# Output projection of a cross-attention layer in three fp32r passes, with reordered selections, maxima and remainders

## The reference

```python
def xattn(query, key, value, mask, ...):      # query = layernorm(x), key = value = ctx
    q = query @ Wq + bq                       # 16 heads of 16
    k = key @ Wk + bk                         # one head of keys and values for all
    v = value @ Wv + bv
    scores = einsum('bhqd,bkd->bhqk', q, k) / sqrt(16)
    scores = where(mask == 0, -1e9, scores)
    x = einsum('bhqk,bkd->bhqd', softmax(scores), v)
    return x @ Wo + bo                        # the output projection

def ffn(x, ...):                              # x = layernorm(x1)
    x_mixed = mix_kernel[0] * previous row + mix_kernel[1] * row + mix_kernel[2] * next row
    h = einsum('bsd,pdm->bspm', x_mixed, W1) + b1             # 9 paths of 64
    stacked = einsum('bspm,pmd->bspd', h, W2) + b2
    idx = argmax(tanh(x_mixed @ Wo1 + bo1) @ Wo2 + bo2)       # one path per row
    return layernorm(x + stacked[idx]) * gamma + beta

x1 = x + xattn(layernorm(x), ctx, ctx, mask)
out = x1 + ffn(layernorm(x1))
```

## Time and profile before

| | before |
|---|---|
| median of 3 runs | 339.88 us (339.84 to 340.29) |
| the profiled execution | 341.15 us, of which the span of instructions is 339.3 us |
| TensorE busy | 306.1 us, 90% of the span |
| VectorE busy | 269.8 us, 80% |
| GpSimd busy | 194.1 us, 57% |
| ScalarE busy | 178.8 us, 53% |
| mean granted TensorE clock | 0.986 |

### The profile page before, as it was taken

The page is one execution under the profiler, slowest core; times in us unless marked ns, Lnnn a source line. Parts: engine busy times, 40 slices in busy tenths (PEclk is TensorE's granted clock), DMA queues, the critical chain, the costliest instruction groups (busy, mean ns, idle before and its releaser), DMA issues. The chain is left out here.

```text
span 339.3 us, 7009 instructions
## 1 busy us (share of the span) xinstructions
PE 306.1 (90%) x2700; PEld 224.0 (66%) x2700; DVE 269.8 (80%) x620; ACT 178.8 (53%) x279; POOL 194.1 (57%) x235
## 2 busy tenths in 40 slices
PE   1688978779899999999999999999999999899991
PEld 1563355365578766795778766795779578766891
DVE  2786698898769797989789797979598868495876
ACT  1354715814861686537842777357462655356620
POOL 0264001493196289925895299827884597519554
PEclk9999699999999999999999999999999999999998
DMA  7942200002002001200120010000100010001003
GB/s 218 231 103 68 77 2 1 2 1 79 3 6 74 2 2 62 77 3 0 65 65 16 0 63 2 2 0 3 64 2 1 0 65 2 0 2 43 22 0 124
DMA packets 20586, 13.14 MB, mean 39 GB/s; under 512 B 10113, under 2 KB 20426, under 8 KB 20554
## 3 DMA queue, kind: packets, MB, share of 16 engines
q1 hardware_dynamic: 18914, 12.14, 11.9%
q10 hardware_dynamic: 1640, 0.57, 0.7%
HBM read 8.51 MB, written 4.19 MB: 37 GB/s over the span
## 5 line engine op out<-in xcount | busy, mean ns | idle before, releaser
L1507 POOL TENSOR_TENSOR rs<-ve,halfneg 128x4 f32<-128x4 f32 x22 | 25.1, 1142 | 80.7 <-DVE ve L1155 80.7
L894 ACT ACTIVATE e<-ps 128x1024 f32<-128x1024 f32 x32 | 31.1, 1023 | 17.6 <-PE ps L577 17.6
L1192 DVE TENSOR_REDUCE mx<-ps 128x16 f32<-128x1024 f32 x32 | 38.0, 1214 | 0.3 <-PE ps L545 0.3
L1595 POOL TENSOR_TENSOR hml<-hs,hmh 128x512 fp32r<-128x512 f32 x28 | 35.0, 1277 | 5.3 <-ACT hmh L956 5.3
L700 PE MATMUL ps<-w2h,hmh 128*128 128x256 f32 (+1 forms) x140 | 35.6, 289 | 0.0
L701 PE MATMUL ps<-w2l,hmh 128*128 128x256 f32 (+1 forms) x140 | 34.6, 283 | 0.0
L946 ACT ACTIVATE hs<-ps,b1s 128x512 f32<-128x512 f32 x28 | 19.3, 689 | 23.4 <-PE ps L452 23.4
L613 PE MATMUL ps<-wo,osb 128*128 128x256 f32 x128 | 31.4, 391 | 0.0
L1312 DVE TENSOR_TENSOR hs<-hs,ps 128x512 f32<-128x512 f32 x28 | 18.5, 681 | 15.7 <-PE ps L680 15.7
L919 ACT ACTIVATE xh<-x,vb,rs 128x256 f32<-128x256 f32 x24 | 12.5, 590 | 33.0 <-POOL vb L1520 33.0
L1560 POOL TENSOR_TENSOR y<-xh2f,gms 128x256 f32<-128x256 f32 x24 | 20.4, 878 | 15.9 <-DVE xh2f L1164 15.9
(11 more groups left out here) (169 smaller groups left out, 772.5 us busy)
## 6 DMA issues: line engine op xcount, KB each, us to landing
xin<-in_x SPq DMA_DIRECT2D x8, 512.0 KB, 3.8
out<-y SPq DMA_DIRECT2D x6, 512.0 KB, 2.8
min_<-in_mask_Bx1xSxS_ik SPq DMA_DIRECT2D x8, 128.0 KB, 4.0
hs<-in_L_ffn_W SPq DMA_DIRECT2D x2, 288.0 KB
hs<-in_L_ffn_W SPq DMA_DIRECT2D x1, 512.0 KB
out<-y SPq DMA_DIRECT2D x2, 256.0 KB, 2.1
out<-xin SPq DMA_DIRECT2D x2, 256.0 KB, 2.3
cst<-in_constants SPq DMA_DIRECT2D x1, 384.0 KB, 6.6
```

Source lines behind the costliest of these rows:

```text
L894: nc.scalar.activation(e[:, 2 * i:2 * i + 2, :], ps[:, bank:bank + 2, :], ACT.Exp).then_inc(s_e, 1)
L1192: v.tensor_reduce(mx[:, k, :].rearrange("p (a h) -> p a h", a=2), ps[:, bank:bank + 2, :].rearrange("p a (h s) -> p a h s", s=SK), AX.X, A ...
L1507: g.tensor_tensor(ln[7][:, :], ln[6][:, :], halfneg[:, :], ALU.pow).then_inc(s_r, 1)
L1595: g.tensor_tensor(L.lo(m, r), L.selected(m, r), L.hi(m, r).bitcast(F32), ALU.subtract).then_inc(L.s_hl, 1)
```

## The change

It does the following:
1. The projection is made in three fp32r passes. Wo is split once (`woh` on ScalarE at the end of step 1, `wol` on GpSimd). The attention output is rounded in halves on ScalarE (`attn_hi`) and its remainder made on VectorE (`attn_lo`); TensorE waits for the one ahead of the first two products of a tile and for the other ahead of the third. They lie in buffers of the tail (`lhh`, `lhl`).
2. On TensorE `rep3` stands ahead of the projection of tiles 0 and 1, and `scores_for_max` of tiles 2 and 3 inside W2, behind the hi products of tiles 0 and 2. On VectorE all selections stand ahead of the first maximum, and the last two maxima behind the x1 sums.
3. GpSimd's remainder of the mix stands behind `rstd2`.
4. In full steps q is rounded on ScalarE, not on VectorE. `keep_xh2` stands behind the roundings of the selections.
5. The variance of the usual layer norms is made by aggregation (`bn_aggr` per tile and two small operations) in place of six operations.

```diff
             def project_out(b, j, tiles):
-                pe.wait_ge(s_oT, at(b, 2 * NJ, 2 * j + tiles[0] // 2 + 1))
+                half = at(b, 2 * NJ, 2 * j + tiles[0] // 2 + 1)
+                if (b, j) == (0, 0):
+                    pe.wait_ge(s_wol, 1)
+                pe.wait_ge(s_oTh, half)
                 for k in tiles:
+                    o, ks = ps[:, k // 2, (k % 2) * D:(k % 2 + 1) * D], slice(k * P, (k + 1) * P)
                     for c in range(KD):
-                        mm = nc.tensor.matmul(ps[:, k // 2, (k % 2) * D:(k % 2 + 1) * D], osb[:, c, k * P:(k + 1) * P],
-                                              wo[:, c, :], start=(c == 0), stop=(c == KD - 1))
+                        nc.tensor.matmul(o, osh[:, c, ks], woh[:, c, :], start=(c == 0), stop=False)
+                        nc.tensor.matmul(o, osh[:, c, ks], wol[:, c, :], start=False, stop=False)
+                    pe.wait_ge(s_oTl, half)
+                    for c in range(KD):
+                        mm = nc.tensor.matmul(o, osl[:, c, ks], woh[:, c, :], start=False, stop=(c == KD - 1))
                 mm.then_inc(s_wo, 1)
...
+            def attn_hi(b, j):
+                for half in range(2):
+                    act.wait_ge(s_oT, at(b, 2 * NJ, 2 * j + half + 1))
+                    t = slice(half * CH // 2, (half + 1) * CH // 2)
+                    nc.scalar.activation(osh[:, :, t], osb[:, :, t], ACT.Copy).then_inc(s_oTh, 1)
...
                 if f:
                     hidden(*f, 2)
                     hidden(*f, 3)
+                    selected_hi(*f, 0)
+                    attn_hi(*n)
+                    for m in range(1, NM):
+                        selected_hi(*f, m)
                     keep_xh2(*f)
-                    for m in range(NM):
-                        selected_hi(*f, m)
...
-                v.tensor_tensor(su, st[:, :, 0, :], st[:, :, 1, :], ALU.add)
-                v.tensor_tensor(dm, st[:, :, 0, 1], st[:, :, 1, 1], ALU.subtract).then_inc(s_halves, 1)
...
+                for k in tiles:
+                    a = v.bn_aggr(ln[1][:, k, :], ln[0][:, k].rearrange("p a c -> p (a c)"))
...
+            def attn_lo(b, j, half):
+                dve.wait_ge(s_oTh, at(b, 2 * NJ, 2 * j + half + 1))
+                t = slice(half * CH // 2, (half + 1) * CH // 2)
+                v.tensor_tensor(osl[:, :, t], osb[:, :, t], osh[:, :, t].bitcast(F32), ALU.subtract).then_inc(s_oTl, 1)
...
-                if f and f[1] == 0:
-                    mixed_lo(f[0], 1)
-                if f and n[1] == NJ - 1:
-                    early_mixed_lo(n[0])
                 if front and front[1] == 0:
                     value_operand(front[0])
...
                 if n:
                     rstd2(*n)
+                if f and f[1] == 0:
+                    mixed_lo(f[0], 1)
+                if f and n[1] == NJ - 1:
+                    early_mixed_lo(n[0])
```

More of the change, by code:

```diff
@@ L174, in layer_program @@
         lhh, lhl = sb("lhh", [P, NM - 1, CH], F32R), sb("lhl", [P, NM - 1 - KD, CH], F32R)
+        osh, osl = lhh[:, 0:KD, :], lhh[:, KD:2 * KD, :]
+        woh, wol = [lhl[:, i, :].rearrange("p (c n) -> p c n", c=KD) for i in range(2)]
         wq32 = h4s[:, :].rearrange("p (c n) -> p c n", c=KD)
@@ L764, in step @@
                 if f:
-                    rep(*f, 3)
-                    if front:
-                        scores_for_max(*front, 2, banks)
                     rep(*f, 4)
@@ L770, in step @@
                     project_out(*n, (2, 3))
-                if f and front:
-                    scores_for_max(*front, 3, banks)
-                if f and front:
-                    w2_tiles(*f, (0, 1, 2, 3))
-                elif f:
+                if f:
                     w2_product(*f, 0, "hi")
                     w2_product(*f, 2, "hi")
+                if f and front:
+                    scores_for_max(*front, 2, banks)
+                    scores_for_max(*front, 3, banks)
+                if f:
                     w2_product(*f, 0, "lo")
@@ L781, in step @@
                     w2_product(*f, 2, "lo")
+                if f and front:
+                    w2_tiles(*f, (3,))
                 if front:
@@ L989, in step @@
                     pv_copy(*n)
+                if front and f:
+                    q_round(*front)
                 if f:
@@ L992, in step @@
                     hidden(*f, 3)
+                    selected_hi(*f, 0)
+                    attn_hi(*n)
+                    for m in range(1, NM):
+                        selected_hi(*f, m)
                     keep_xh2(*f)
-                    for m in range(NM):
-                        selected_hi(*f, m)
                 if after and not f:
                     layernorm1_apply(*after)
+                if n and not f:
+                    attn_hi(*n)
                 if late and not f:
@@ L1001, in step @@
                     copies_t1(*after, 6, False, 1)
+                    act.wait_ge(s_wo_in, 32)
+                    nc.scalar.activation(woh, wo[:, :, :], ACT.Copy).then_inc(s_woh, 1)
                 if f:
+                    act.wait_ge(s_xh2f, at(f[0], NJ, f[1] + 1))
                     layernorm2_apply(*n)
@@ L1232, in x1_stats @@
                 if half:
-                    variance(ln2, (s_ln2s, s_ln2h, s_ln2p, s_ln2v), c, 2 * c, -1.0)
+                    variance(ln2, (s_ln2s, s_ln2p, s_ln2v), c, 2 * c, -1.0)
             def mix(b, j, last, sems):
@@ L1340, in residual_stats @@
                 if half:
-                    variance(ln3, (s_ln3s, s_ln3h, s_ln3p, s_ln3v), c, 2 * c)
+                    variance(ln3, (s_ln3s, s_ln3p, s_ln3v), c, 2 * c)
             def tail_variance(i, stats, sign=1.0):
@@ L1373, in step @@
                     early_mix(n[0])
-                if front:
+                if front and not f:
                     q_round(*front)
@@ L1391, in step @@
                     select(*f, 1)
+                if n:
+                    attn_lo(*n, 0)
+                if f:
                     select(*f, 2)
+                if n:
+                    attn_lo(*n, 1)
+                if f:
+                    select(*f, 3)
+                    select(*f, 4)
                     if front:
@@ L1395, in step @@
                         take_max(*front, 1, banks)
-                    select(*f, 3)
-                    select(*f, 4)
-                    if front:
-                        take_max(*front, 2, banks)
                     if n:
@@ L1403, in step @@
                     if front:
+                        take_max(*front, 2, banks)
                         take_max(*front, 3, banks)
```

30 lines of the change are left out of this document (16 added, 14 removed).

## The result

The changed kernel takes 346.34 us (median of 4 runs, 345.44 to 348.2), the kernel before 339.86 us beside it (339.34 to 340.29). The ratio is 1.0199, with a 95% interval of 1.0169 to 1.023: slower, by about 2% (the interval has 2% in its middle). The prediction was 349.4 us, with a range of 339.5 to 354.0.

What follows compares the result with a forecast made beforehand. TensorE, 90% busy, waits on VectorE's chain to the variance, which has 0.8 us of cover. 6.0 (full steps) + 2.8 (steps 2, 3) + 0.7 (step 9) = 9.5 on 341.15 gives 350.6, less 1.27: 349.4 us, range 339.5 to 354.0.

Steps and rivals of the forecast that it cites:

- the two mechanisms: VectorE's two-input operations wait for GpSimd passes at two places per full step: attention remainders, 0.9 us; maxima split, +0.34 us.
- rival 1: VectorE's attention remainders don't wait for GpSimd, only the split of the maxima does: +4.3 us, 344.2 us; chance 0.20.
- TensorE's saving: Three-pass projection on TensorE: 0.75 us less per chunk, 6.0 us over 8 at most, swallowed by waiting for the maxima.
- s: Instant in a step when TensorE spreads the inverse denominators; the forecast counts the step's later events from it.
- x: Instant when VectorE ends the second layer norm's variance: s + 11.2 without any collision, s + 12.1 forecast.
- First collision: Full step, ahead of the variance: VectorE's two attention remainders wait for GpSimd's selection remainders, 0.9 us, bounds 0 and 2.5.
- Second collision: Full step, behind the variance: the maxima split waits for GpSimd's moved mix remainder, +0.34 us, bounds -0.7 and about +0.8.
- A full step: A step with selections and scores (steps 4 to 8): 0.9 + 0.34 = 1.2 us longer, +6.0 us for five.
- Steps 2 and 3: Steps without selections: both attention remainders precede VectorE's last two maxima, +1.4 us each, +2.8; bounds per step -0.75 and +2.2.
- Step 9: The step without scores, where every delay of the variance counts in full: +0.7 us, within -0.3 and +1.6.
- Rival 2: VectorE goes first each time and GpSimd waits: -0.9 us, 339.0 us, or 334.7 with TensorE's saving; chance 0.20.
- Rival 3: A later maxima split delays following work into the next step, some 1.2 us more in four steps: 354 us; chance 0.10.

Runs made afterwards that it cites:

- e4: The changed kernel with GpSimd's remainder of the selections made for 16 of 512 columns only, from the second chunk on: 344.11 us in one run.
- e1: The changed kernel with GpSimd's remainder of the mix back at the front of its step: 343.37 us.
- e8: The changed kernel with VectorE's two attention remainders ahead of selections 1 to 4, the mix remainder left where the change puts it: 345.37 us.
- e5: e1 with VectorE's two attention remainders ahead of selections 1 to 4 and replications 3 and 4 behind the projection's first half: 341.71 us.
- e9: e6 with the residual and its statistics one maximum earlier on VectorE, and the fourth score tile behind W2's second tile: 338.05 us.
- e6: e5 with the first batch's output projections in fp32, without attention rounding and remainders there: 339.27 us.
- e3: The changed kernel with the projection in plain fp32, without the roundings and remainders of the attention output: 342.58 us.
- e7: e3 with GpSimd's remainder of the mix at the front of its step: 339.08 us.
- e2: The kernel before with the three-pass projection alone, its roundings and remainders included, everything else in the old order: 352.51 us.
- e10: e7 with the residual and its statistics one maximum earlier on VectorE, and the fourth score tile behind W2's second tile: 341.05 us.

## Why the prediction was right, and where it was off

The direction and the two mechanisms were right, most sizes too large. By the time alone this would not show: 346.3 us lies nearer to rival 1's 344.2 than to the forecast's 349.4, and only the rows tell the two apart.

1. **TensorE's saving is swallowed.** Right. Busy time fell by 4.8 us (6.0 at most was forecast), and 1.30 us of waiting stands ahead of the maxima's transposition (about 1.5 forecast). TensorE got there at s + 14.80, where s + 14.6 was forecast.
2. **x without collision at s + 11.2.** e4 has 11.33.
3. **First collision, +0.9 us: mis-sized.** The waits that I walked out, 0.25 and 0.65, were 0.25 and 0.54 (0.93 and 1.22 less 0.68). Of their 0.79, x saw 0.54: in e4, where the remainders are free, VectorE has to wait for the last selection's replication and begins it 0.83 us after the one before, not 0.60. How long such a wait is can be read off: the twelve remainders of steps 4 to 9 lasted longer than 0.68 by the rest of the GpSimd pass that ran when they began, less 0.13 or 0.14 us (0.39 us left, 0.25 longer; 0.67 left, 0.54 longer), and so did the subtraction of the maxima (1.09 left, 0.95 longer than 0.42). In two of the five full steps, which the forecast's walk did not look at, the pass that the first remainder meets is the last addition of the output bias: 1.01 and 1.19 us in place of 0.93 and 1.22, x at s + 11.93. The Trainium skill's page "SBUF — State Buffer", section "🔬 SBUF: two separate sides", has the shared port pair as an exclusive lock; the traces agree: the second remainder ends 0.56 after GpSimd's pass does (180.13 and 179.57), about the 0.60 us of one such operation, and falls to 0.68 in e4.
4. **Second collision, +0.34 us: mis-sized.** The order of events was as forecast (the cast behind the first pass, the subtraction behind the second), but GpSimd's mix passes began at x + 1.34 and not 1.55, mostly because its product for the layer norm took 0.20 and not the 0.35 of the earlier trace rows, and the subtraction ended at x + 4.18 and not 4.45. The transposition came at x + 4.47, not x + 4.75. That is +0.06 over before. Against a kernel with the mix in front it is worth 0.41 us in three full steps and 0.79 in two (e1), or 0.75 to 0.79 in all five (e8 against e5), which my comparison with before did not make visible.
5. **A full step, +1.2 us each.** It was +0.81 on average, five times, so 4.0 and not 6.0. This is the largest error. Of it x accounts for 0.72 in three steps (the collision's 0.54, and the 0.18 by which e4's x is later than before's) and for 0.78 in two, the split for 0.06.
6. **Steps 2 and 3, +1.4 each.** Right for step 2, mis-sized for step 3: the maxima's transposition came 1.38 and 0.97 later. In step 3 the remainders cost the forecast's 1.4, but GpSimd's additions came later too, as the forecast had them, and so the cast of the maxima no longer met one: it took 0.29 us in place of 0.72. The forecast did not draw that conclusion.
7. **Step 9, +0.7.** It was +0.45: the remainders put 1.99 us on the chain (2.1 forecast), and 0.80 of idle time and 0.79 of the variance went (0.7 and 0.65 forecast), so x moved by 0.40.
8. **Not in the sum:** the first spread came at 42.41 and not 44.04. The rows put this down to TensorE's clock. In the profiled execution of before it was at half (1.2 GHz) from 32.83 to 39.66, in that of the changed kernel from 34.03 to 37.44, then again from 44.27 to 47.68. TensorE had been busy 2.23 of the 3.43 us ahead of the first stretch in the one and 2.25 of 3.43 in the other. e9 has the long stretch too (32.86 to 39.69) and its first spread at 43.89; in the other ten kernels, the changed one among them, 3.41 us at half clock lie ahead of the first spread, and it comes at 41.58 to 42.83. So this term belongs to the execution and not to the change. The windows 32.8 to 39.7 and 44.2 to 47.7 of before (busy time and count by engine, granted clock, DMA share, GB/s):
```profile
32.80:39.70 6.90, 6.66 (x30) 1.12 (x32) 4.76 (x6) 5.32 (x7) 1.76 (x3) 0.51 0.33 95
44.20:47.70 3.50, 2.86 (x26) 2.17 (x27) 3.50 (x5) 0.00 (x0) 0.00 (x0) 1.00 0.02 5
```
and of the changed kernel:
```profile
32.80:39.70 6.90, 6.66 (x86) 2.44 (x88) 4.84 (x6) 6.59 (x9) 3.21 (x3) 0.75 0.35 95
44.20:47.70 3.50, 3.09 (x16) 2.74 (x17) 3.40 (x6) 1.23 (x2) 0.00 (x0) 0.51 0.00 0
```
The second stretch cost it nothing: e5 has none there and the same step 2 (14.89 us to the second transposition). From the second transpositions to the next spreads 0.5 us was saved in all.

The parts give -1.63 + 1.29 + 1.02 + 4.04 + 0.45 - 0.48 = 4.7 us, the difference of the two spans (the 1.29 and 1.02 are steps 2 and 3 up to the second transposition). The medians differ by 6.5, because the profiled run of before was 1.3 us above its median and that of the changed kernel 0.5 below. Without the clock's -1.63 the parts give 6.3, close to the medians; no trace shows whether the other executions of before lack the long stretch.

**The rivals.** Rival 1 (no first collision) falls with the 0.93 and 1.22 us and e4. Rival 2 (VectorE first, 339.0) falls with the same rows and the split's 0.47 and 1.38; e5 comes nearest to building it, by order, with 341.71; e6 reaches 339.27 only because it also takes the three passes out of the first batch. Rival 3 (the delay is carried on) falls: the time behind the second transposition did not grow (item 8).

**What each part costs, by the runs.** The mix remainder's later place costs 3.0 us (e1), 3.5 (e3 against e7) or 3.7 (e5 against e8). The three passes cost 4.3 us in the new order with the mix in front (e1 against e7), 3.8 with it late (changed against e3), and 13.0 in the old order (e2). e5 and e8 ran in one job, and so did e2 and its kernel before. The other pairs ran in two jobs, between which the kernel before moved by up to 0.4 us, and their figures are no surer than that. The new order, together with the aggregated variance and the rounding of q on ScalarE, is about level (e7, -0.3), and no run takes these three apart. It is what makes the three passes bearable. That the mix remainder's place is nearly half of the loss, and a half that the three passes do not need, was not in the prediction.

## What to carry to other kernels

Before work is taken off the busiest engine, find what ends last ahead of its next wait and give that chain nothing: here 0.6 us of TensorE per chunk (4.8 us over eight) was bought with two remainders on VectorE, whose 1.2 us a moved maximum made room for, and with 0.5 us of waiting for GpSimd, for which nothing did. When two-input work of VectorE and passes of GpSimd alternate, lay both out on one time line; a pass that is moved meets whatever stands at its new place, and another pass may stand beside the operation that was to be freed (the bias additions of e5 and e8, in every other step). Take such an edit apart into its moves, since one of them may cost as much as the whole (the mix remainder) and another pay for itself only together with the rest (the order).

## What the runs showed of the hardware

- A VectorE operation with both operands in SBUF that begins while a GpSimd pass runs takes longer by the rest of that pass less 0.13 or 0.14 us: so in all twelve remainders of steps 4 to 9 of the changed kernel, in those of e1 and e2, and in e5 and e8 where a bias pass ran (0.68 us left, 1.23 in place of 0.68). One with an operand in PSUM took no longer: the selections kept 0.67 to 0.68 us beside the same passes.
- GpSimd loses as well: its four bias passes took 3.27 us beside VectorE's remainders and 2.86 alone, and a remainder of the selections took 1.55 and not 1.29 where it began beside one of VectorE's.
- TensorE's granted clock was at 1.2 GHz in one to four stretches of every profiled run ahead of the final one, each 3.41 us long, except one of 6.83 us in before, e4 and e9. The first began at 21.3 to 22.5 us in four kernels and at 32.8 to 34.6 in the others, later ones at 43 to 46, 69 to 77, 107 or 284 us. One in step 9 of e10, where TensorE had been busy 2.16 of the 3.40 us ahead of it, goes with 1.6 us more (14.64 against e7's 13.06); one in step 2 of the changed kernel with none.
- A lone score tile between W2's products cost TensorE 0.30 us more than one of a pair, with no idle time recorded: 15.21 against 15.51 us from the spread to the maxima's transposition (e7, e10), 14.64 against 14.94 (e6, e9).
